# Perceiver layer on one core: the cross part in steps of single groups, and the filler products of TensorE taken out

## What is computed

```python
# cross part, once
y = layernorm(x)
y = layernorm(y + attention(y, y, y, causal), g1, beta1)             # 32 x 32 scores
y = layernorm(y + attention(y, ctx, ctx), g2, beta2)                 # 32 x 257 scores
x = x + layernorm(y + relu(y @ w1 + b1) @ w2 + b2, g3, beta3)        # 128 -> 512 -> 128
# token part: r = layernorm(x), then 2 layers, each
h = rmsnorm(r); q, k, v = silu(h @ Wq), silu(h @ Wk), silu(h @ Wv)   # 8 heads of 16; q, k normalised
r = r + rmsnorm(delta_rule(q, k, v, beta)) @ Wo                      # S += beta * k (v - S k), o = S q
r = r + (silu(rmsnorm(r) @ Wg1) * (rmsnorm(r) @ Wg2)) @ Wd           # 128 -> 352 -> 128
x = x + rmsnorm(r)
x = x + experts(layernorm(x))         # 8 of 32 by sigmoid gate, from 4 of 8 groups, and shared ones
```

## Time and profile before

| | |
|---|---|
| runs (3) | 760.36, 762.5, 763.86 us |
| profiled execution | 763.72 us, span 761.9 us |
| mean granted TensorE clock | 0.853 |
| TensorE busy | 625.3 us (82%) |
| VectorE busy | 461.8 us (61%) |
| ScalarE busy | 256.4 us (34%) |
| GpSimd busy | 97.1 us (13%) |
| cross part | 0 to about 112 us |
| data back from DRAM | about 124 us |

### The profile page before, as it was taken

The page is one execution under the profiler, slowest core; times in us unless marked ns, Lnnn a source line. Parts: engine busy times, 40 slices in busy tenths (PEclk is TensorE's granted clock), DMA queues, the critical chain, the costliest instruction groups (busy, mean ns, idle before and its releaser), DMA issues.

```text
span 761.9 us, 15678 instructions
## 1 busy us (share of the span) xinstructions
PE 625.3 (82%) x6640; PEld 427.1 (56%) x6640; DVE 461.8 (61%) x1124; ACT 256.4 (34%) x555; POOL 97.1 (13%) x140
## 2 busy tenths in 40 slices
PE   2777951786899999694997699978888799999995
PEld 1434641475688858464796678776444344444442
DVE  5846694978966354748828822475556855555552
ACT  1455510742421623642632034214323122222221
POOL 2535452300000001301100001010011000000000
PEclk9888985955599999897768658976899999999998
DMA  9994021000000000000000050000032163333321
GB/s 343 291 375 160 1 83 29 0 2 2 2 3 4 3 1 3 0 3 0 2 3 2 2 178 2 2 2 1 0 80 65 57 161 94 96 97 108 88 81 28
DMA packets 18981, 46.68 MB, mean 61 GB/s; under 512 B 3456, under 2 KB 8192, under 8 KB 18656
## 3 DMA queue, kind: packets, MB, share of 16 engines
q1 hardware_dynamic: 18368, 45.43, 19.3%
q10 hardware_dynamic: 544, 0.26, 0.1%
HBM read 43.32 MB, written 2.36 MB: 60 GB/s over the span
## 4 chain that ended last, share of the span: by engine, by line
PE 66%; DVE 22%; ACT 3%; DMA 3%; POOL 2%; issue 2%; SPq 1%; DVEq 0%; POOLq 0%
PE psum L753 7%; PE psum L748 7%; PE psum L758 7%; PE psum L685 5%; PE psum L594 5%; PE psum L560 3%; PE psum L711 3%; PE psum L714 3%; PE psum L674 3%; PE psum L621 3%; PE psum L667 2%; PE psum L720 2%; PE psum L571 2%; DVE yr L1287 2%; PE psum L464 2%; DVE pcT L1287 2%
## 5 line engine op out<-in xcount | busy, mean ns | idle before, releaser
L932 ACT ACTIVATE arena<-psum 128x512 f32<-128x512 f32 x68 | 40.6, 598 | 136.0 <-PE psum L748 122.9
L1363 DVE TENSOR_TENSOR arena<-psum,arena 128x512 f32<-128x512 f32 x64 | 44.2, 691 | 59.6 <-PE psum L753 57.8
L758 PE MATMUL psum<-arena,wed_sb 128*128 128x512 f32 x128 | 66.8, 604 | 0.0
L776 ACT ACTIVATE arena<-psum 128x512 f32<-128x512 f32 x56 | 33.3, 600 | 69.7 <-PE psum L560 41.0
L1368 DVE TENSOR_TENSOR arena<-arena 128x512 f32<-128x512 f32 x64 | 44.3, 692 | 14.0 <-PE psum L758 13.8
L560 PE MATMUL psum<-arena 32*64 32x128 f32 x1024 | 41.9, 327 | 6.6 <-ACT arena L776 2.8
L952 POOL TENSOR_TENSOR ve<-ss,eps_rms 128x4 f32<-128x4 f32 x16 | 3.7, 230 | 340.5 <-ACT yr L827 252.9
L560 PEld LDWEIGHTS psum<-arena 32*64 32x64 f32 x1024 | 36.8, 165 | 12.6 <-ACT arena L776 4.1
L753 PE MATMUL psum<-yT,weu_sb 128*128 128x512 f32 x68 | 36.3, 616 | 7.9 <-DVE arena L1363 7.9
L758 PEld LDWEIGHTS psum<-arena,wed_sb 128*128 128x128 f32 x128 | 24.6, 192 | 31.3 <-issue 22.7
L1314 DVE TENSOR_TENSOR arena<-psum,small 128x1024 f32<-128x1024 f32 x24 | 28.2, 1214 | 14.2 <-PE psum L667 14.2
(11 more groups left out here) (283 smaller groups left out, 1290.2 us busy)
## 6 DMA issues: line engine op xcount, KB each, us to landing
arena<-shares SPq DMA_DIRECT2D x64, 256.0 KB, 3.9
arena<-in_ctx_t SPq DMA_DIRECT2D x16, 514.0 KB, 8.9
arena<-in_ctx_z SPq DMA_DIRECT2D x16, 512.0 KB, 10.5
XA<-in_x SPq DMA_DIRECT2D x1, 1024.0 KB, 5.1
zlast<-in_ctx_last SPq DMA_DIRECT2D x4, 256.0 KB, 17.7
x_mid<-XA SPq DMA_DIRECT2D x4, 256.0 KB, 3.0
weg_sb<-in_we_gate SPq DMA_DIRECT2D x2, 512.0 KB, 6.5
weu_sb<-in_we_up SPq DMA_DIRECT2D x2, 512.0 KB, 7.5
```

Of the source, the lines that this page charges most:

```text
L758: pe.matmul(x3, wed_sb[:, (p - 1) % (NPAIR + 1), :], act_a[pr], start=(p == 0), stop=False, skip_group_check=True).then_inc(x_down[pr], 1)
L776: return act.activation(out_, in_, ACT.Copy, scale=scale)
L932: act.activation(act_g[pr], banks[4 * pr + 2 * (n % 2)], ACT.Silu).then_inc(x_silu[pr], 1)
L1363: dve.tensor_tensor(act_gu[pr], banks[4 * pr + 1], act_g[pr], ALU.mult).then_inc(x_gu[pr], 1)
```

## The change

1. The cross part's list is made of single groups. Each pair has five chains: `BEFORE` (`st0` to `nm1`, and `ev1`, the eviction behind `nm1`) for each of its groups, ten `c` steps, and `AFTER` (`cr`, `nm2`, `ev2`, `up`, `dn`, `nm3`, `fin`) for each of its groups. `XTURNS` merges the ten chains: a, b and v, w are `BEFORE` of groups 0, 1 and 2, 3; c and x the `c` steps of pair A and B; d, e and y, z `AFTER` of groups 0, 1 and 2, 3.
2. Semaphore values are no longer written as sums of constants; `count` takes them from the list. `a_var` and the norm of `nm0` go into `a_vec`, `at_max` and the first `at_pT` into `at_vec`.
3. PSUM banks: a group has a low bank (bank + u) and a high one (bank + 2 + u). `nm0` and `nm1` transpose into the high one, `nm2` into the low one; `up` alternates between both, `dn` uses the high one.
4. New waits: the first `c` product of a pair waits for `ev1` of its second group, `up` of a pair's first group for the last copy of the probabilities, GpSimd's addition to XA for the group's `nm0`.
5. In the token part both calls of `dense` are gone.

The diff, cut to its core:

```diff
-XTURNS = "AABAABABBABAAAAAABABABABAABABBAABBBABBBABABBBB"
+BEFORE = ["st0", "nm0", "sas", "sap", "sar", "nm1", "ev1"]
+AFTER = ["cr", "nm2", "ev2", "up", "dn", "nm3", "fin"]
+XTURNS = ("ababwvaavabvbaawbccvbvbcwcccwvvdcwxcxccdwwexdxxxydxdeyeyxdexxdzyezyyzyeezzzz")
...
+    for pr, (g0, g1, steps, h0, h1) in enumerate(("abcde", "vwxyz")):
+        for u, name in ((0, g0), (1, g1)):
+            chains[name] = iter([(kind, u, pr) for kind in BEFORE])
+        chains[steps] = iter([("c", n, pr) for n in range(NU * GT + 2)])
+        for u, name in ((0, h0), (1, h1)):
+            chains[name] = iter([(kind, u, pr) for kind in AFTER])
+    return [next(chains[turn]) for turn in XTURNS]
...
@@ TensorE, cross part
+                        if m == 0:
+                            pe.wait_ge(a_yT[pr], count("yT", pr, "ev1", 1))
...
+                elif kind == "up":
+                    pe.wait_ge(w_in, N_WEIGHT)
+                    pe.wait_ge(a_yT[pr], count("yT", pr, "ev2", u))
+                    if u == 0:
+                        pe.wait_ge(at_pT[pr], NT)
+                    for c in range(FFC):
+                        if c >= 2:
+                            pe.wait_ge(ff_h[pr], count("h", pr, kind, u) - FFC + c - 1)
+                        pe.matmul((high, low)[c % 2], w1_sb[:, c * P:(c + 1) * P], zT[g][:, :],
+                                  start=True, stop=True).then_inc(ff_up[pr], 1)
...
@@ TensorE, token part
                     elif kind == "lout":
-                        if u == 0:
-                            dense(banks[bank + 2], 8)
                         pe.wait_ge(l_inv, pi + 1)
...
                     elif kind == "otr":
-                        if u == 0:
-                            pe.wait_ge(s_ocp[u], pi + 1)
-                            dense(b0, 6)
                         pe.wait_ge(o_n, i + 1)
...
@@ GpSimd, nm2 of one group
+                        x_g = gcols(XA, g).rearrange("p (j c) -> p j c", j=GT)
+                        pool.wait_ge(a_vec[pr], count("var", pr, "nm0", u))
+                        pool.tensor_tensor(x_g, x_g, bc(rowv[:, BE3:BE3 + 1, :], [P, GT, D]),
+                                           ALU.add).then_inc(a_scaled[pr], 1)
```

More of the change, by code:

```diff
@@ L91, in cross_schedule, with count @@
 def cross_schedule():
-    streams = [iter(CROSS), iter(CROSS)]
-    return [(next(streams["AB".index(turn)]), "AB".index(turn)) for turn in XTURNS]
-XSTEPS = cross_schedule()
+    chains = {}
+    for pr, (g0, g1, steps, h0, h1) in enumerate(("abcde", "vwxyz")):
[5 more added lines that the diff above has]
+    return [next(chains[turn]) for turn in XTURNS]
+XSTEPS = cross_schedule()
+ONCE = lambda *kinds: {kind: 1 for kind in kinds}
+SIGNALS = {"var": ONCE("st0", "nm0", "sar", "cr", "dn"), "rstd": ONCE("st0", "sar", "cr", "dn"),
+           "norm": ONCE("nm1", "nm2"), "scaled": {"nm1": 1, "nm2": 3}, "tr": ONCE("nm0", "nm1", "nm2", "c"),
+           "yT": ONCE("nm0", "ev1", "ev2"), "scores": ONCE("sas", "c"), "max": ONCE("sas", "sap", "c"), "exp": ONCE("sas", "c"),
+           "pT": ONCE("c"), "out": ONCE("sap", "c"), "read": ONCE("cr"), "up": {"up": FFC},
+           "h": {"up": FFC}, "ff": ONCE("dn"), "done": ONCE("fin")}
+SIGNALLING = {"scores": (0, 8), "max": (0, 8), "exp": (0, 8), "tr": (1, 9), "pT": (1, 9), "out": (2, 10)}
+def count(name, pr, kind, u):
+    total = 0
+    for k, v, p in XSTEPS:
+        if p == pr and k in SIGNALS[name] and (k != "c" or v in range(*SIGNALLING[name])):
+            total += SIGNALS[name][k]
+        if (k, v, p) == (kind, u, pr):
+            break
+    return total
 def schedule():
@@ new lines, in _ @@
+                if kind == "c":
+                    n = u
+                    if n < NT:
+                        act.wait_ge(at_vec[pr], count("max", pr, kind, n))
+                        if pr == 1:
+                            act.wait_ge(ca_read[0], count("read", 0, "cr", n // GT))
+                        act.activation(pc[:, n, :], banks[bank + n % 2][:, 0:KEYS], ACT.Exp, bias=nmax[pr][:, n:n + 1],
+                                       accum_out=rsum[pr][:, n:n + 1]).then_inc(at_exp[pr], 1)
+                    if 1 <= n <= NT:
+                        act.wait_ge(a_tr[pr], count("tr", pr, kind, n))
+                        copy(pcT[:, n - 1, :], banks[bank + 2][:, 0:2 * P]).then_inc(at_pT[pr], 1)
+                    continue
@@ L1104, in _ @@
             st = Steps(dve, d_steps)
-            for kind, pr in XSTEPS:
+            done = [None] * NG
+            for kind, u, pr in XSTEPS:
                 bank = 4 * pr
-                if kind[0] == "c" and kind[1] != "r":
-                    n = int(kind[1:])
+                if kind == "c":
+                    n = u
                     if n < NT:
-                        dve.wait_ge(at_scores[pr], NU + n + 1)
+                        dve.wait_ge(at_scores[pr], count("scores", pr, kind, n))
```

341 lines of the change are left out of this document (151 added, 190 removed).

## The result

The changed kernel takes 773.0 us (median of 4 runs, 770.2 to 775.6) against 762.5 us: 1.0137 times as long, 95% interval 1.0099 to 1.0174. Forecast was 757. The profiled execution took 773.7 us (span 771.9).

A forecast was written before the change was run, and what follows sets the result against it. TensorE, busy 82% of the span with 66% of the chain, was taken as the bound; 763.7 - 1.1 (cross part) - 4.3 (filler) = 758.3 for the profiled execution, 757 for the median, range 746 to 768.

The forecast's parts named there:

- the cross part's term of -1.1 us: New order of the cross part: end -0.6 and way home -0.5, together -1.1 us; bounds -8 and +5.
- The filler's term of -4.3: Token layers: giving up 56 filler products sums to -4.3 us, the clock's fall near 250 included.
- First "up" at 68.1: Cross part: group 0's first "up" product starts at 68.1 instead of 68.85; 64.1 without the VectorE-GpSimd port meeting.
- The stall before group 3's transposes: Cross part's feed-forward stretch: TensorE waits about 3 us for group 3's norm, bounds 0 and 5.
- The stretch behind "up" as a whole: Cross part, first "up" to last "down": 35.6 us of work plus a 3.0 us stall, from 68.1 to 106.7.
- my bound for none of them: Cross part without port meeting and stall: 7.5 us less, used in a rival of 746 us, chance 0.2.
- The end: End of the cross part: one group finishes in about 4.4 us instead of two in 6.6.
- The way home: Copies home after the cross part: -0.5 us, bounds 0 and -1.6; group 1's earlier finish hides most of pair 0's issues.
- the prediction's own sign of being wrong: Cross part moving by more than 5 us, or granted clock past 262 staying at 0.5.
- The rival "the order costs": Cross part: GpSimd holds VectorE at cr of groups 1 and 3 and the fins; +5, total 763; chance 0.15.
- The filler's own places: Token layers: 243 and 249 together +3.6 us, 370 -1.7, 442 and 453 -6.0, 524 -0.2; layer 0 worth 0.
- The rival "the clock does not come back": Token layers: without filler TensorE stays at 1.2 GHz from 250 to 271 and behind 455; +13.4, total 770; chance 0.15.

The follow-up runs named there:

- e6: Changed kernel with GpSimd's affines of groups 0 and 2 placed later and group 1's last two VectorE steps earlier; 762.6 us against 763.7 for the kernel before.
- e5: Changed kernel with group 1's last two VectorE steps moved in front of group 2's down product's addition; 764.2 us against 763.7 for the kernel before.
- e3: Changed kernel with GpSimd's four operations behind each group's second normalization on one tile of four, output incomplete; 762.0 us against 764.0 for the kernel before.
- e1: Kernel before with all filler products given up and the old cross-part order kept; 763.9 us against 764.0 for the kernel before.
- e8: Kernel before with filler kept up to 370 us, given up at 442, 453 and 524 us; 757.0 us against 763.3.
- e10: Changed kernel with GpSimd's affines later, group 1's last VectorE steps early, filler kept up to 370 us; 761.9 us against 763.3 for the kernel before.
- e11: e10 with the layers' six weight loads moved behind the context loads; 754.4 us against 763.3 for the kernel before.
- e7: Kernel before with filler kept in layer 0 and given up in layer 1; 755.6 us against 763.3.

## Why the prediction was wrong

The step that failed is the cross part's term of -1.1 us: it measured +8.5. The overlap of VectorE and GpSimd was counted on the path for two passes where three stood there, slack on TensorE was taken as free, and the way home was taken as hidden. The filler's term of -4.3 failed as well: the rest grew by 1.5, as the clock changed elsewhere. Of the 16 us between forecast and result the first is 9.6 and the second 5.8.

- *First "up" at 68.1: wrong, 71.1.* The meeting in group 1's second pass was called: 4.93 us against 5.02 in the old row. And e6 confirms the start without it (64.6, against the stated 64.1). What failed is "TensorE has about 4 us of slack there, so nothing before 48.4 counts": group 1's first pass starts at 57.28, not about 54.9, behind a pause of 3.84 us at 38.6 and 3.6 us at half clock after it. e5, with 1.6 us less of the pause, was 2.0 us earlier at "up". 3.0 us. What makes the pause is open.
- *The stall before group 3's transposes: right in size, 3.86 against 3.0, in part by luck.* The reciprocal root was to stand behind the affines in GpSimd's queue; GpSimd was idle ahead of it. What held group 3 was VectorE: group 0's last pass (5.30 us, not priced) directly ahead of its residual, and then its own 4.22. *The stretch behind "up" as a whole: wrong*, 71.09 to 113.58 = 42.5 us instead of 38.6. I treated the stall as a time that only shifts. The granted clock behind it was 0.71, and 1.00 from 91.9 to 95.6, and "down" of group 2 took 5.25 instead of 3.73 us (1.5). Another 0.9 is the stall itself. The last 1.5 are in the base: e3, without stall or fall, takes 37.0 us for the stretch (66.72 to 103.70), where I had 35.6 after taking out all idle time of the old order. e3 puts all meetings of the two engines at 9.7 us at the mark; my bound for none of them was 7.5, and its own terms (68.1 - 64.1, and 3.0) give only 7.0.
- *The end: right in its own size* (4.6 us from the last "down" to the last write, against 4.4). *The way home: wrong.* "Group 1 finishes about 8 us before group 3, and that hides most of them": its last write came only 5.9 us before group 3's (112.3 and 118.2), as its steps stand behind group 2's, and sixteen issues take 6.1. Home cost +2.1 instead of -0.5; e5 took it back, and more (11.9 us against 16.9).
- Sum of the cross part: 3.0 + 3.9 + 0.2 + 2.6 = 9.7 us later than said, and 8.5 instead of -1.1 (9.6) measured. *This is the step that turned the sign*, and it meets the prediction's own sign of being wrong, a cross part moved by more than 5 us. The rival "the order costs" named its mechanism and stopped at 763.
- *The filler's own places: right in sum, and 249 in its mechanism.* Read between the two traces, 249 cost +4.0 (said +3.6, half clock over 128 instructions and a projection, 7.04 us against 3.88), 370 gave 1.4 (1.7), 442 and 453 together 5.2 (6.0), 524 gave 1.6 (0.2): -4.2 against -4.3, though 524's miss and the others cancel by luck.
- *The filler's total: wrong.* I took it that the clock changes nowhere else. It does: 2.8 us between 396 and 444, 0.9 before 160 us and about 1.8 behind 540. e1 puts the total at nothing. I had looked for the filler's worth where each group stood, and that is not where layer 0's pays.
- *The rival "the clock does not come back" (770)* had the time nearly right by another way, which is luck: in the changed kernel's trace the clock did come back at 271 and behind the projection (0.95 from 471 to 480). As a mechanism it is real, e8 and e10 show it.

## What to carry to other kernels

When an order of steps is changed by hand, list for each queue which other engine works at the same time on the same kind of operand, and price every such meeting on the chain, not the first alone; then ask what each new stall does to the clock of what follows. Give an engine its own order where its work is not urgent: moving GpSimd's affines out from beside the VectorE passes they slowed brought 7 us with no operation changed. Judge fillers one place at a time, and run each choice several times: by the rests, half of them were worth 7 us and the other half cost as much, and the same program did not always take the same course. Profile an unchanged part more than once before reading a few us at its end.

## What the runs showed of the hardware

- Four VectorE operations of three inputs on 128 x 128 take 1.14 us beside a quiet GpSimd and 3.3 to 5.3 us beside one that runs its own of 1.27 us; GpSimd's own stay at 1.26 to 1.32 us in the rows shown. In the changed kernel each slow one ended about 0.15 us after an operation of GpSimd's, one for one. The same VectorE operation with an input in PSUM was never slowed, not even beside a GpSimd at work (89.24 us in the changed kernel): 0.32 to 0.35 us each in all 17 profiles, against up to 1.44 us for those with all tiles in SBUF.
- TensorE stayed at half clock for nearly 48 us (granted 0.53) though it was 97% busy, most of it with products of 64 x 32: 256 instructions took 13.87 us in e10 and in e11, against 7.88 us in e7 (granted 0.98). The times of e8, e10 and e11 fall into two kinds 8 to 13 us apart from run to run.
- The same work, from an XA update to the squares behind the first pair's state products of layer 1, took 45.0, 47.4, 48.2 or 50.2 us in 17 profiles and nothing between; the mean granted clock was 0.77, 0.76, 0.71 and 0.69. Fillers up to 200 us earlier went with the shorter lengths, but one profile without any had 48.24.
- TensorE can pause 2.0 to 3.8 us in the middle of a row of like products with no wait on record: in eight of eight profiles of the new order with early weight loads, while in the changed kernel the DMA engines were full (mean share 1.02), and in none of the three with later loads. The old order had equally full DMA engines and no pause.
